# Band products one tile in every pair, their reads issued by GpSimd, in a fused attention and feed-forward layer

## The reference

```
qh = qh / sqrt(16)
scores = einsum('bhid,bhjd->bhij', qh, kh)
rel    = clip(pos[None, :] - pos[:, None], -64, 64) + 64
bias_r = einsum('bhid,rd->bhir', qh, rel_pe)          # rel_pe (129, 16)
bias   = take_along_axis(bias_r, rel)                 # differs by column only in a band of 129 diagonals
attn   = softmax(scores + bias); out = attn @ vh
x = layernorm(x + out @ out_w.T + out_b)
x = layernorm(x + ffn(x))                             # ffn: gelu, weights alpha * sign(w)
```

## Time and profile before

| | |
|---|---|
| median of three runs | 2521.58 us |
| profiled execution, and its span | 2522.68 us, 2521.0 us |
| attention, full steps | about 361 to 2057 us |
| third stage | about 2156 to 2521 us |
| TensorE busy in the span | 2256.5 us (90%) |
| VectorE, ScalarE, GpSimd busy | 1737.7, 1660.6, 628.0 us |

### The profile page before, as it was taken

How to read it: one execution, slowest core, us unless ns; L and a number is a source line. 1 busy time by engine, 2 the same in 40 slices (tenths; PEclk the granted TensorE clock), 3 DMA queues, 4 the chain that set the end, 5 groups by cost and what they waited for, 6 DMA issues and landing times. The chain is left out here.

```text
span 2521.0 us, 46743 instructions
## 1 busy us (share of the span) xinstructions
PE 2256.5 (90%) x14642; PEld 1243.9 (49%) x14642; DVE 1737.7 (69%) x3444; ACT 1660.6 (66%) x1983; POOL 628.0 (25%) x1117
## 2 busy tenths in 40 slices
PE   4996579999999999999999999999999999699997
PEld 3564234444444444444444444444444444488886
DVE  2443457777777777777777777777777775488885
ACT  2432157777777777777777777777777777466676
POOL 0001111122111221212212122221222210466673
PEclk9999579999999999999999999999999999899999
DMA  6997767777767777777777777777777762333321
GB/s 193 364 341 276 183 175 192 192 199 202 194 190 195 197 202 193 195 194 197 201 191 196 195 197 198 195 197 194 191 202 196 197 191 76 108 96 108 109 78 43
DMA packets 452027, 468.57 MB, mean 186 GB/s; under 512 B 106901, under 2 KB 410726, under 8 KB 451942
## 3 DMA queue, kind: packets, MB, share of 16 engines
q1 hardware_dynamic: 355830, 368.91, 49.9%
q0 software_dynamic: 83072, 89.92, 15.1%
q10 hardware_dynamic: 13040, 8.80, 1.1%
HBM read 244.73 MB, written 221.25 MB: 185 GB/s over the span
## 5 line engine op out<-in xcount | busy, mean ns | idle before, releaser
L890 ACT ACTIVATE probs<-weigh_ps 128x1024 f32<-128x1024 f32 x1024 | 1047.4, 1023 | 377.0 <-PE weigh_ps L1058 375.6
L1018 PE MATMUL ring_ps<-keys,queries 48*128 48x512 f32 x2048 | 832.6, 463 | 28.7 <-DVE partial_max L931 18.7
L942 DVE CUSTOM_DVE_ANT_1 ring_ps<-ring_ps,band_all 128x512 f32<-128x512 f32 x1008 | 680.7, 715 | 229.8 <-PE ring_ps L1018 229.5
L931 DVE TENSOR_REDUCE partial_max<-ring_ps 128x2 f32<-128x1024 f32 x512 | 627.7, 1226 | 285.5 <-PE ring_ps L1018 240.7
L1058 PE MATMUL weigh_ps<-queries,keys 50*128 50x512 f32 (+3 forms) x2688 | 735.4, 379 | 0.9 <-ACT probs L890 0.5
L1075 PE MATMUL sum_ps<-probs,values 128*32 128x512 f32 x4096 | 547.5, 606 | 0.1
L1018 PEld LDWEIGHTS ring_ps<-keys,queries 48*128 48x128 f32 x2048 | 363.9, 187 | 353.3 <-issue 170.9
L1043 PE MATMUL weigh_ps<-ident,band_all 128*128 128x128 f32 x2048 | 362.6, 290 | 126.1 <-ACT carried L878 113.1
L878 ACT ACTIVATE carried<-weigh_ps 128x1024 f32<-128x1024 f32 x256 | 261.9, 1024 | 190.2 <-PE weigh_ps L1006 167.3
L1043 PEld LDWEIGHTS weigh_ps<-ident,band_all 128*128 128x128 f32 x2048 | 216.9, 141 | 325.2 <-ACT carried L878 189.2
L1058 PEld LDWEIGHTS weigh_ps<-queries,keys 50*128 50x128 f32 x2688 | 358.3, 186 | 17.0 <-ACT probs L890 8.9
(11 more groups left out here) (113 smaller groups left out, 1744.7 us busy)
## 6 DMA issues: line engine op xcount, KB each, us to landing
band_scr<-carried SPq DMA_DIRECT2D x256, 512.0 KB, 5.1
band_all<-band_scr SPq DMA_DIRECT2D x128, 512.0 KB, 4.4
band_all<-band_scr SPq DMA_DIRECT2D x128, 256.0 KB, 3.3
keys<-k_scr POOLq DMA_DIRECT2D x128, 240.0 KB, 8.5
k_scr<-k_parts SPq DMA_DIRECT2D x16, 1792.0 KB, 8.4
q_scr<-q_parts SPq DMA_DIRECT2D x16, 1024.0 KB, 6.3
queries<-q_scr POOLq DMA_DIRECT2D x128, 128.0 KB, 3.1
o_scr<-weighted_s SPq DMA_DIRECT2D x64, 256.0 KB, 5.8
```

The lines of the kernel that those rows point to most:

```text
L890: nc.scalar.activation(probs[:, u % PROBS], weigh_ps[weigh_of["scores", at]][:], ACT.Exp).then_inc(s_pr, 1)
L931: nc.vector.reduce_max(partial_max[:, g, :, e, 0], ring_ps[:, first:second + 1], AX_X).then_inc(s_seen, HG)
L942: nc.vector.tensor_tensor_reduce(out=both, in0=both, in1=bias, scale=1.0, scalar=LOWEST, op0=ALU.add, op1=ALU.max, accum_out=partial_max[: ...
L1018: nc.tensor.matmul(dst, query_rows(c, h, ROWS, tile * P, (tile + 1) * P), key_rows(c, h, ROWS, c0, c0 + 512), start=True, stop=True, tile_ ...
```

## The change

1. `band_product` makes one tile (two matmuls) in every pair of the step, where it made two tiles in pairs 4 to 7. The first tile of a step's bands is still made in pair 4, the last in pair 3 of the next step. `copy_band` copies half as much (512 elements in each partition instead of 1024), eight times a step.
2. In a pair, `band_product` stands ahead of `lagging`.
3. The two PSUM buffers are now counted as three uses in every pair, so that each pair alternates scores, band, scores.
4. SyncE only writes chunks, at units 3, 7, 11 and 15, when both tiles are copied. GpSimd reads them: one after the first row maxima, one after the loads of keys and values, two after the second row maxima. Before each read it waits for the write to land.
5. The row maxima are turned at units 4 and 10 (pairs 2 and 5, the third and sixth) instead of 8 and 12, and SyncE loads them there. The order of the two heads in a look follows from that.

```diff
-            TURN_AT = {8: 0, 12: 1}
+            TURN_AT = {4: 0, 10: 1}
...
             def bands_at(step, m):
-                return m >= QT and 0 <= step + BAND_STEPS < G
+                return 0 <= band_index(step, m) < G * NT
...
             def band_index(step, m):
-                return (step + BAND_STEPS) * NM + m - QT
+                return (step + BAND_STEPS) * NT + m - QT
...
-                            look_heads[n] = (1, 0) if m % 2 == 0 and u % 2 == 0 and not turns_at(step, u) else (0, 1)
+                            look_heads[n] = (1, 0) if u % 2 == 0 and (m % 2 == 0) != turns_at(step, u) else (0, 1)
...
-                        if what[0] == "scores" or m >= QT:
-                            weighs += 1
+                        weighs += 1
...
             @block.sync
             def _(sp):
                 def write_bands(i, n):
                     c, m = n // NM, n % NM
-                    sp.wait_ge(s_be, cnt(i, NM, n + 1))
+                    sp.wait_ge(s_be, cnt(i, NT, 2 * n + 2))
...
-                def read_bands(i, n):
...
                 def unit(i, step, u):
                     m = u // 2
+                    if turns_at(step, u):
+                        load_minus_max(i, step, TURN_AT[u])
                     if u == 5 and step > 0:
                         store_sums(i, step - 1)
-                    if u == 9 and turns_at(step, 8):
-                        load_minus_max(i, step, 0)
-                    if u == 13 and turns_at(step, 12):
-                        load_minus_max(i, step, 1)
-                    if u == 0 and bands_at(step - 1, NT - 1):
-                        read_bands(i, band_index(step - 1, NT - 1))
-                    if u % 2 and bands_at(step, m):
-                        if bands_at(step, m - 1):
-                            read_bands(i, band_index(step, m - 1))
-                        write_bands(i, band_index(step, m))
+                    if u % 4 == 3:
+                        chunk = band_index(step, m) // 2
+                        if 0 <= chunk < G * NM:
+                            write_bands(i, chunk)
...
             @block.gpsimd
             def _(pool):
+                def read_bands(i, n):
+                    c, m = n // NM, n % NM
+                    pool.wait_ge(s_bw[n % BANDS_OUT], cnt(i, 16 * NM // BANDS_OUT, 16 * (n // BANDS_OUT + 1)))
...
+                def read_chunk(i, step, quarter):
+                    chunk = (step + BAND_STEPS) * NM + quarter - 3
+                    if 0 <= chunk < G * NM:
+                        read_bands(i, chunk)
+
                 def step_of(i, step):
                     if 0 <= step and step + 3 < G:
                         if step > 0:
                             pool.wait_ge(s_sc, cnt(i, 2 * UNITS, step * 2 * UNITS))
                         load_queries(pool, i, step + 3)
-                    if step + 1 < G:
+                    if 0 <= step + 1 < G:
                         minus_maxima(i, step, 0)
+                    read_chunk(i, step, 0)
                     if 0 <= step and step + 3 < G:
                         if step > 0:
                             pool.wait_ge(s_av, cnt(i, NT, step * NT))
                         load_keys(pool, i, step + 3)
                         load_values(pool, i, step + 3)
-                    if step + 1 < G:
+                    read_chunk(i, step, 1)
+                    if 0 <= step + 1 < G:
                         minus_maxima(i, step, 1)
+                    read_chunk(i, step, 2)
+                    read_chunk(i, step, 3)
...
                 def copy_band(i, n):
+                    chunk, e = n // 2, n % 2
+                    act.wait_ge(s_bp, cnt(i, NT, n + 1))
+                    if e == 0 and chunk >= BANDS_OUT:
+                        act.wait_ge(s_bw[chunk % BANDS_OUT], cnt(i, 16 * NM // BANDS_OUT, 16 * (chunk // BANDS_OUT)))
+                    nc.scalar.activation(band_out[:, chunk % BANDS_OUT, :, e], weigh_ps[weigh_of["band", n]][:, :, 0:2 * P],
+                                         ACT.Copy).then_inc(s_be, 1)
...
                     products(i, step, m, 0)
-                    lagging(i, step, m)
                     if bands_at(step, m):
                         band_product(i, band_index(step, m))
+                    lagging(i, step, m)
```

More of the change, by code:

```diff
@@ L722, in write_bands @@
                                  ).then_inc(s_bw[n % BANDS_OUT], 16)
-                def read_bands(i, n):
-                    c, m = n // NM, n % NM
-                    sp.wait_ge(s_bw[n % BANDS_OUT], cnt(i, 16 * NM // BANDS_OUT, 16 * (n // BANDS_OUT + 1)))
-                    def read(e, c0, c1, offset):
-                        sp.dma_start(band[:, c % SLOTS, m, :, e, c0:c1],
-                                     flat(band_scr, band_base(c, m) + e * P * BAND_ROW + offset,
-                                          [[BAND_ROW - 1, P], [2 * P * BAND_ROW, HG], [1, c1 - c0]])
-                                     ).then_inc(s_b[m], 16)
-                    if m == 0:
-                        read(0, HALF, 2 * P, HALF)
-                        read(1, 0, 2 * P, 0)
-                    elif m == NM - 1:
-                        read(0, 0, 2 * P, 0)
-                        read(1, 0, P, 0)
-                        read(1, P, P + HALF, 2 * P)
-                    else:
-                        sp.dma_start(band[:, c % SLOTS, m].rearrange("p h e c -> p (h e) c"),
-                                     flat(band_scr, band_base(c, m), [[BAND_ROW - 1, P], [P * BAND_ROW, HG * 2], [1, 2 * P]])
-                                     ).then_inc(s_b[m], 16)
                 def load_minus_max(i, step, g):
@@ L810, in _, with read @@
             def _(pool):
+                def read_bands(i, n):
+                    c, m = n // NM, n % NM
+                    pool.wait_ge(s_bw[n % BANDS_OUT], cnt(i, 16 * NM // BANDS_OUT, 16 * (n // BANDS_OUT + 1)))
+                    pool.sem_inc(s_passed, 1)
+                    def read(e, c0, c1, offset):
+                        pool.dma_start(band[:, c % SLOTS, m, :, e, c0:c1],
+                                     flat(band_scr, band_base(c, m) + e * P * BAND_ROW + offset,
+                                          [[BAND_ROW - 1, P], [2 * P * BAND_ROW, HG], [1, c1 - c0]])
+                                     ).then_inc(s_b[m], 16)
+                    if m == 0:
+                        read(0, HALF, 2 * P, HALF)
+                        read(1, 0, 2 * P, 0)
+                    elif m == NM - 1:
+                        read(0, 0, 2 * P, 0)
+                        read(1, 0, P, 0)
+                        read(1, P, P + HALF, 2 * P)
+                    else:
+                        pool.dma_start(band[:, c % SLOTS, m].rearrange("p h e c -> p (h e) c"),
+                                     flat(band_scr, band_base(c, m), [[BAND_ROW - 1, P], [P * BAND_ROW, HG * 2], [1, 2 * P]])
+                                     ).then_inc(s_b[m], 16)
                 def minus_maxima(i, step, g):
@@ L850, in _ @@
                 pool.wait_ge(s_set, 6)
-                for step in range(-1, FIRST):
+                for step in range(-START, FIRST):
                     step_of(0, step)
@@ L984, in wait_for @@
                         else:
-                            pe.wait_ge(s_be, cnt(i, NM, n + 1))
+                            pe.wait_ge(s_be, cnt(i, NT, n + 1))
                 def seen_count(n):
@@ L995, in band_product @@
                 def band_product(i, n):
-                    c, m = n // NM, n % NM
-                    if m == 0:
+                    c, tile = n // NT, n % NT
+                    if tile == 0:
                         pe.wait_ge(s_q[c % SLOTS], i * (16 * LOADS) + 16 * LOADS * (c // SLOTS + 1))
@@ L1000, in band_product @@
                     dst = weigh_ps[weigh_of["band", n]]
-                    for e in range(2):
-                        tile = 2 * m + e
-                        for h in range(HG):
-                            table = rel_terms[h * ROW_TILE:h * ROW_TILE + ROWS, :].rearrange("p (a c) -> p a c", a=3)
-                            moving = table[:, 0:3:2] if tile == NT - 1 else table[:, 0:2]
-                            last = nc.tensor.matmul(dst[:, h, e * 2 * P:(e + 1) * 2 * P].rearrange("p (a c) -> p a c", a=2),
-                                                    query_rows(c, h, ROWS, tile * P, (tile + 1) * P), moving,
-                                                    start=True, stop=True, tile_position=(h * ROW_TILE, 0))
+                    for h in range(HG):
+                        table = rel_terms[h * ROW_TILE:h * ROW_TILE + ROWS, :].rearrange("p (a c) -> p a c", a=3)
+                        moving = table[:, 0:3:2] if tile == NT - 1 else table[:, 0:2]
+                        last = nc.tensor.matmul(dst[:, h, 0:2 * P].rearrange("p (a c) -> p a c", a=2),
+                                                query_rows(c, h, ROWS, tile * P, (tile + 1) * P), moving,
```

(1 more changed line is left out.)

9 lines of the change are left out of this document (2 added, 7 removed).

## The result

The changed kernel took 2437.65 us (median of four runs, 2435.95 to 2438.35) against 2521.09 us for the kernel before on the same chip: a ratio of 0.9657, 95% interval 0.9628 to 0.9686. That is 83 us less where 125 were forecast; it lies in the range and on the side forecast, 42 us above the forecast itself. The profiled execution has a span of 2435.4 us, 85.6 us less than before.

The account below looks back on a forecast made before the run. TensorE was taken as the bound, 28.74 us a step including a 1.85 us wait for the band copy. A step of 26.8 us saves 118 us over 61 steps, the prologue 9: 2396 us, range 2350 to 2472.

Parts of the forecast that it names:

- The wait: TensorE's transposes opening the next scores wait for ScalarE's band copy, 1.85 us a step; all of it was to go.
- The band product: Eight half products ahead of the weighted sums, 1.72 us a step, 1.4 of it hidden: 26.5 us a step.
- The row of before: Profile of the kernel before: bands cost 2.54 us a step, 1.85 the wait, so 1.03 of 1.72 us of products hidden.
- What is late next: Part 1 wants the buffer part 0's exponential reads; ScalarE's extra copies make pair 1's exponential late: 0.3 us a step charged.
- Row maxima: Second set turned in pair 5: ready after 2.58 us, TensorE there after 2.66, a tie; no charge.
- Reads on GpSimd: Seven DMAs a step, 6.2 us at most on GpSimd; cost nothing while writes land in 8.5 us.
- The lock: GpSimd issues no read while a VectorE instruction runs: 30 us back, 2426 us; chance 0.02, inside the stall rival's.
- The prologue: Before step 0 SyncE no longer waits for landings, 12.5 us go; first read 0 to 5 us later: -9 us.
- Nothing is hidden: Rival: half products add in full to TensorE's step, 27.93 us a step, 2464 us; chance 0.17.
- everything: Rival: ring waits in every pair absorb the band products, 26.21 us a step, 2356 us; chance 0.12.
- The exchange: Rival: part 1 waits for part 0's exponential, 0.23 us in every pair; only the prologue gains, 2511 us; chance 0.04.
- The stall of the turn behind a landing: Rival: GpSimd, held by a write's landing, delays pair 5's turn on TensorE, 3.8 us a step, 2628 us; chance 0.08.

Follow-up runs that it names:

- the copy first and turns at 6 and 12: Changed kernel with ScalarE's band copy ahead of its copy of the sums in pair 1, row maxima turned at units 6 and 12: 2412.01 us, ratio 0.9569.
- the bare one: Not a run: the step without band products near the end of the kernel before (pairs 1 to 7 of step 61, pair 0 of step 62), measured once: 26.2 us.
- the band copy first: Changed kernel with ScalarE's band copy in pair 1 ahead of its copy of the sums, nothing else: 2417.06 us, ratio 0.9596.
- the second turn at 12: Changed kernel with ScalarE's band copy ahead of its copy of the sums and the second row maxima turned at unit 12 instead of 10: 2415.40 us, ratio 0.9580.
- write-first reads: Changed kernel with band reads on SyncE instead of GpSimd, each chunk read after the next one's write is issued: 2433.43 us, ratio 0.9649.

## Why the prediction came out as it did

**The wait.** Right in the main. At the matmuls 106.3 us went to 19.5, and the shrunken copy (0.59 us) came in time in all pairs but one, where the wait should have vanished from the list.

**The band product: the term that was mis-sized.** I let 1.4 of 1.72 us be hidden and charged 0.3. With the copy first and turns at 6 and 12 no matmul waits for `carried`, and the step is 27.01 - 26.2 = 0.8 us above the bare one: 0.9 of 1.72 is hidden. Doubling the product says much the same: 0.74 of another 1.76 shows. The row of before had said 1.03 of 1.72; the step that failed was "small pieces in all eight pairs should hide at least as much", with its 0.16 us hidden in each of seven pairs. That is 0.5 us a step, 30 us.

The table shows that the 0.8 is not spread. Pairs 1 and 5 pay 0.24 and 0.26 us, the product's whole time, pair 0 pays 0.19, and pairs 2, 6 and 7 pay nothing or next to it (in pairs 3 and 4 a turn moved, so they do not tell). The bare stretch fits this. The two looks between the sums of pairs 0 and 1 stand 0.34 us apart (those of pair 5 too), without a wait into which a product could go. Between the sums of pairs 1 and 2 they stand 0.49 apart, and the second one's weight load waits for VectorE:

```profile
2085.80 0.50 PE L1018 MATMUL ring_ps<-keys,queries 48*128 48x512 f32 x1
2086.14 0.39 PE L1018 MATMUL ring_ps<-keys,queries 48*128 48x512 f32 x1
...
2088.72 0.50 PE L1018 MATMUL ring_ps<-keys,queries 48*128 48x512 f32 x1
...
2089.21 0.18 PEld L1018 LDWEIGHTS ring_ps<-keys,queries 48*128 48x128 f32 x1 [0.20 <-DVE partial_max L931]
```

So the prediction read one pair's wait and took it for all. Why pair 0 pays, and why a second product costs pairs 1 and 5 only about 0.13, stays open.

**What is late next.** The 0.3 us for ScalarE in pair 1 was right in size and place: the band copy first gives back 0.32. The mechanism was not quite mine, and the short waits for `probs` that I named as a sign did not come (TensorE's matmuls waited 0.7 us in all for them from 400 to 2050 us). I expected the exponential of part 1 to end late; it was the band copy behind the copy of the sums. The sums end later than before because the product now stands ahead of them.

**Row maxima.** Charged at nothing, by a tie. GpSimd holds the turn's weight load by 22.1 us in all, which I had named as a sign of being wrong. It weighs little: with the second turn at 12 this wait is gone and the step only 0.05 us shorter. The places cost 0.11 us a step against turns at 6 and 12, 7 us by the steps, which the run times alone do not tell apart. The cost of a turn itself was already in the bare step.

Set against the forecast of 26.8, the step is 26.2 + 0.8 + 0.32 + 0.11 = 27.43, where 0.3, 0.3 and nothing had been added to 26.2. That this meets the 27.44 measured proves nothing, since the 0.8 is itself what is left of the 27.01; only the 0.32 and the 0.11 are differences between runs that one edit parts.

**Reads on GpSimd.** Cost nothing, as predicted: seven DMAs at 725 to 798 ns, within my bound of 0.88, reads of 6.6 us that nobody waits for. I did not see what the move was for. Had the reads stayed in SyncE's list in the old order, the new kernel would have lost everything (2576.51 us); I had looked at that list only for the prologue. There four writes, each behind the landing of the one before, no longer fit into every step.

**The rule of the Trainium skill** that plain loads belong to SyncE ("DMA: Bandwidth & Descriptors", section "Issuing engine by pattern"): write-first reads by SyncE took 4 us less than by GpSimd, the way of the rule, but the intervals overlap, so that no run here shows it. The same reads in the other order are 139 us slower, which the rule does not bear on.

**The lock.** The seven reads of a step take 0.73 to 0.80 us each with VectorE busy 154 of 200 us, no longer than the 0.88 of a load beside an idle VectorE. No lock of the size that I priced shows.

**The prologue.** -9 forecast, -9.65 measured; VectorE starts 3 us later (281.41, with the first read at 275.53), inside the 0 to 5, and SyncE loads the row maxima at once:

```profile
298.32 0.27 ACT L889 ACTIVATE minus_max<-ring_ps 16x128 fp32r<-16x128 f32 x1 [1.69 <-PE ring_ps L1030]
298.61 1.30 SPq L729 DMA_DIRECT2D queries<-minus_max  x2
```

**The rivals.** "Nothing is hidden" gave 2464 and "everything" 2356; the measured half lies between, and the time is nearer to the first (26 us) than to my 2396 (42 us). The range held because it took in both. The exchange did not come: TensorE's matmuls hardly wait for an exponential. The stall of the turn behind a landing did not come either: writes land in 4.0 us at the median, and GpSimd had read and stood 3.05 us idle when the second row maxima came:

```profile
1020.74 0.78 POOL L803 DMA_DIRECT2D band_all<-band_scr  x1 [2.66 <-DMA band_scr<-carried]
1024.57 0.20 POOL L811 TENSOR_TENSOR negative<-zero,row_max 128x8 f32<-128x8 f32 x1 [3.05 <-DVE row_max L956]
```

## What to carry to other kernels

Where a measured row says how much of a piece of work is hidden, keep it: that smaller pieces hide better was only an argument, and the row was nearer. Then look in which pairs the hiding wait stands, before counting it in all. In a queue that issues in order, put nothing that must leave on time behind a wait for a landing; turning round two lines was worth 143 us, and moving them to another engine no more than that. And when a wait is removed, look in the same place for which instruction stands ahead of the released one on the slower engine: here one more exchange gave 20 us.

## What the runs showed of the hardware

- The same reads make fewer DMA packets when GpSimd issues them: 335,292 in the whole run against 452,028 with write-first reads on SyncE, for the same 468.58 MB, with no difference in time that can be told.
- The landing of a transfer depends on what was issued just before it. A 512 KB read from SyncE took 4.2 us at the median ahead of each write, and 10.3 us right behind a fresh write. From GpSimd it took 6.6 us.
- The timeline gives two 256-column matmuls 0.22 us, but two more of them in a pair lengthened it by 0.13 us at the most.
- Sixty-four more matmuls in a loop's body brought a stall of TensorE of 3.1 to 4.7 us in each turn of the loop. Behind one of them eight weighted sums took 1.93 instead of 1.07 us, at a granted clock of 0.56.
- After a stall of 2.78 us one of TensorE's 512-column matmuls took 0.79 instead of 0.50 us, and the granted clock fell from 1.00 to 0.66 for 3.6 us.
